# The three middle batches of a two-layer conditional kernel: one hardware loop, or the same code written out three times

## The chip, the cores and the metric

The kernel runs on one core of one Trainium2 chip. The metric is the device time of one execution in microseconds (us). A core has five instruction streams: PE (TensorE, matmuls), ACT (ScalarE), DVE (VectorE), POOL (GpSimd) and SP (SyncE, which here issues nearly all DMAs). Each stream runs in its own order and waits for the others by semaphores.

## What is computed

For each of 4 batches `x` is 1024 tokens x 512 features, float32. Cut to what matters:

```python
# layer 0: MLP whose last 128 output columns come from one of 16 experts, chosen per batch
h = gelu(x @ fc1_w.T + fc1_b)                    # 512 -> 2048
shared = h @ fc2_w.T + fc2_b                     # 2048 -> 384
expert = h @ experts_w[indices].T + experts_b[indices]   # 2048 -> 128
x = x + concat([shared, expert], -1)
# layer 1: attention pooling, mask chosen per batch by prompt type (prefix, postfix, all but self)
scores = tanh(x @ W1 + b1) @ v
p = softmax(where(mask, scores[:, None, :], NEG_INF), -1)
x = x + (p @ x) / count(mask)
```

## The kernel before, in words

Every float32 factor is split into a high part `hi` (ACT, a copy that rounds) and a remainder `lo` (DVE, a subtraction), and each product is three matmuls of 128x512 (`three`, L699 to L701). fc1 is computed in pairs of 128 hidden rows by a seven-product scheme. The seven products of a pair are P1, P5, P6, P3, P7, P2, P4; they are accumulated in two PSUM banks, `hA` and `hF`, which ACT copies out (`snap`), DVE adds to (`add`, L1278) and ACT puts through GELU (`gelu`, L926).

A batch has 8 pair steps (p = 0 to 7), in which PE does the fc1 products of pair p for the first token half and the second, and between them fc2 (`fc2`, bank `y`) for the hidden rows of the pair before, in eight groups of three matmuls; then 16 unit steps with fc2 alone for the second half. The attention of the batch before is spread over the pair steps as tasks. All four engines have a place for each task in tables written by hand (`POST_P`, `EX_P` and so on), and each engine's order is fixed by them.

The part that matters below is the expert weights. While batch b is computed, the expert matrix of batch b+1 is read in four quarters: SP issues the load into `exth` (`load_ex`, L398, 256 KB), ACT writes the high part to `Ph` (L872), DVE the low part to `Pl` (L1106), SP writes both to the DRAM buffer `exs` (`put_ex`, L406), and only then loads the next quarter. `EX_P` places the quarters in the loop at pair step 0, place 0; step 0, place 1; step 1, place 1; step 1, place 2. In each engine's order these tasks stand ahead of work of the pair itself: DVE's low part of quarter 0 ahead of the first `add` of step 0, ACT's high part of quarter 1 ahead of the third and fourth GELU of step 0, for which P1 of step 1 waits (`gelu_done`), and quarter 3 ahead of the copy of `hA` in step 2.

On SP these loads stand in one queue with the weight loads of the pairs (`load_w1`, L364) and of fc2 (`load_w2`, L368 and L369), and each of those waits until PE has finished with the buffer: before quarter 1 is put and the next loaded, SP waits in `gate` for the fourth fc2 group (group 3) of the pair step.

The program has three bodies: `first` (batch 0, with all weights split on the way), `loop` (batches 1 to 3) and `tail` (attention of the last batch). Before the change `loop` is one hardware loop whose counter `b` lies in a register of each engine: the value of nearly every wait in it, such as `b * 56 + 3`, is computed by register instructions, and so are the DRAM addresses with `b` in them.

Of the kernel before, what the change touches and what calls it, by code (L numbers as in the profile page):

```python
# [4 lines left out]
NB, SEQ, D = 4, 1024, 512  # L5
# [157 lines left out]
def build(nc, x, tok_e, tok_t, fc1_w, fc2_w, exp_w, exp_b, W1, biases, out):  # L163
# [7 lines left out]
    with ctx:  # L171
# [136 lines left out]
        def run(eng, part):  # L308

            part("first", 0)  # L310
            with eng.Fori(1, NB) as b:
                part("loop", b)
            part("tail", NB)

# [34 lines left out]
        def _(sp):  # L349
# [209 lines left out]
            for n in range(4):  # L559
                load_w2raw(n, e)  # L560
            run(sp, part)

            for i in range(OUTS):
# [11 lines left out]
        def _(pool):  # L575
# [75 lines left out]
            def part(kind, b):  # L651
# [31 lines left out]
                for p in range(PAIRS):  # L683
                    for k in range(3):
                        for task, pos in LOOP["p", p, k]:
                            if task[0] == "pool":
# [3 lines left out]
                                                        ALU.add).then_inc(row_sum, 1)  # L690

            run(pool, part)


        @block.tensor
        def _(pe):
# [153 lines left out]
            def part(kind, b):  # L850
# [9 lines left out]
                for u in range(HC):  # L860
                    for oc in range(OC):
                        fc2(kind, b, HC - 2 + u, oc)
                    for task, pos in BODIES[kind]["u", u, 0]:
                        job(kind, b, "u", task, pos)

            run(pe, part)


# [555 lines left out]
```

## Time and profile before

| | us |
|---|---|
| median of 3 runs | 875.6 |
| lowest, highest run | 871.32, 876.32 |
| time of the profiled execution | 868.85 |
| its span (first to last instruction) | 867.1 |
| PE busy in it | 799.7 (92%) |

The span of the profiled execution is the time from its first instruction to its last; 1.75 us of its time lie around it. The times of three executions differ by 0.6%, and the profiled one was below all of them. A busy PE is not a PE at its peak, since the ends of matmuls are modelled: in the stretches where nothing is waited for, a matmul of 512 columns follows the one before it every 0.227 us, though each is shown as 0.39 us long. In the trace batch 1 begins on PE at 185.0 us, batch 2 at 395.9, batch 3 at 607.05, and the last matmul of its fc2 is at 820.0.

### The profile page before, as it was taken

The page shows a single profiled execution, that of the slowest core. Times are in us where ns is not written, and L with a number is a line of the kernel's source. Part 1 is how long each engine was busy: PE and PEld are TensorE (multiplying, and loading weights), DVE is VectorE, ACT ScalarE, POOL GpSimd, SP SyncE. Part 2 cuts the span into 40 slices and gives each one's busy share as a digit, 9 for nine tenths or more (in the row PEclk, how much of TensorE's full clock was granted, in tenths as well). Part 3 has the DMA queues.
Part 4 walks back from the last instruction along what each step waited for, and adds up shares of the span by engine and source line. Part 5 has one row for each costly group of instructions (what it writes and reads, how often), then busy time and mean ns, then how long its engine had stood idle before and what let it go on. Part 6 is the DMA issues. An engine that isn't in the chain of part 4 may idle for free.

```text
span 867.1 us, 12247 instructions
## 1 busy us (share of the span) xinstructions
PE 799.7 (92%) x3550; PEld 648.0 (75%) x3550; DVE 399.1 (46%) x681; ACT 374.1 (43%) x621; POOL 104.9 (12%) x165
## 2 busy tenths in 40 slices
PE   6799999997799999997979999999797999999976
PEld 4677788875678888886758888887685888888755
DVE  6655558533343333761425333456143433275464
ACT  5755656423335434442435523443242553354222
POOL 3463110010000120002000021000200002100160
PEclk9999999998999999999989999999998999999968
DMA  8499988675544468866655447877564456786502
GB/s 265 149 358 356 290 292 276 211 216 185 180 148 135 158 206 282 269 185 214 184 142 169 150 159 235 290 214 219 184 196 145 134 168 209 228 270 210 179 0 98
DMA packets 130583, 176.80 MB, mean 204 GB/s; under 512 B 10048, under 2 KB 97616, under 8 KB 130512
## 3 DMA queue, kind: packets, MB, share of 16 engines
q1 hardware_dynamic: 130352, 175.94, 63.9%
q8 instruction: 33, 0.54, 0.3%
q14 instruction: 38, 0.31, 0.1%
q0 software_dynamic: 160, 0.01, 0.1%
HBM read 136.07 MB, written 39.85 MB: 203 GB/s over the span
## 4 chain that ended last, share of the span: by engine, by line
PE 79%; DMA 5%; DVE 4%; issue 4%; ACT 4%; SPq 3%; ACTq 0%; DVEq 0%
PE y L699 12%; PE y L701 12%; PE y L700 12%; PE hA L699 6%; PE hA L701 6%; PE hA L700 6%; PE hF L699 4%; PE hF L700 4%; PE hF L701 4%; DMA exth<-in_experts_w 4%; PE j L699 2%; PE j L700 2%; PE j L701 2%; PE j L769 1%; ACT gb L926 1%
## 5 line engine op out<-in xcount | busy, mean ns | idle before, releaser
L699 PE MATMUL y<-hs,w2c 128*128 128x512 f32 x512 | 202.7, 396 | 1.0 <-DVE w2c L1106 1.0
L701 PE MATMUL y<-hs,w2c 128*128 128x512 f32 x512 | 200.5, 392 | 0.0
L700 PE MATMUL y<-hs,w2c 128*128 128x512 f32 x512 | 200.5, 392 | 0.0
L699 PE MATMUL hA<-xch,w1c 128*128 128x512 f32 x252 | 103.1, 409 | 42.3 <-ACT gb L872 15.7
L699 PEld LDWEIGHTS y<-hs,w2c 128*128 128x128 f32 x512 | 97.0, 189 | 22.0 <-DVE hs L1106 1.4
L701 PEld LDWEIGHTS y<-hs,w2c 128*128 128x128 f32 x512 | 96.8, 189 | 20.7
L700 PEld LDWEIGHTS y<-hs,w2c 128*128 128x128 f32 x512 | 97.0, 189 | 19.7
L701 PE MATMUL hA<-xch,w1c 128*128 128x512 f32 x252 | 100.6, 399 | 0.0
L700 PE MATMUL hA<-xcl,w1c 128*128 128x512 f32 x252 | 100.6, 399 | 0.0
L699 PEld LDWEIGHTS hA<-xch,w1c 128*128 128x128 f32 x252 | 48.8, 194 | 58.1 <-issue 20.7
L699 PE MATMUL hF<-xch,w1c 128*128 128x512 f32 x190 | 77.4, 407 | 7.8 <-DVE hst L1278 7.8
L700 PE MATMUL hF<-xcl,w1c 128*128 128x512 f32 x190 | 76.0, 400 | 0.0
L701 PE MATMUL hF<-xch,w1c 128*128 128x512 f32 x190 | 76.0, 400 | 0.0
L1106 DVE TENSOR_TENSOR hs<-gb,hs 128x512 fp32r<-128x512 f32 x64 | 44.3, 693 | 67.4 <-ACT hs L872 67.4
L689 POOL TENSOR_TENSOR x1T<-x1T,xnl 128x512 f32<-128x512 f32 x24 | 30.8, 1286 | 355.0 <-DVE x1T L1224 355.0
L926 ACT ACTIVATE hst<-hst,bcol 128x512 f32<-128x512 f32 x62 | 43.3, 718 | 67.7 <-DVE hst L1278 67.7
L1106 DVE TENSOR_TENSOR hs<-hst,hs 128x512 fp32r<-128x512 f32 x64 | 44.1, 689 | 37.8 <-ACT hs L872 37.4
L872 ACT ACTIVATE hs<-hst 128x512 fp32r<-128x512 f32 x64 | 40.3, 629 | 48.1 <-PE y L701 48.1
L701 PEld LDWEIGHTS hA<-xch,w1c 128*128 128x128 f32 x252 | 48.7, 193 | 10.6
L700 PEld LDWEIGHTS hA<-xcl,w1c 128*128 128x128 f32 x252 | 48.9, 194 | 9.4
L1106 DVE TENSOR_TENSOR Pl<-exth,Ph 128x512 fp32r<-128x512 f32 x16 | 12.9, 806 | 83.5 <-ACT Ph L872 83.5
L926 ACT ACTIVATE gb<-gb,bcol 128x512 f32<-128x512 f32 x31 | 22.4, 724 | 66.0 <-DVE gb L1278 66.0
(232 smaller groups left out, 1104.8 us busy)
## 6 DMA issues: line engine op xcount, KB each, us to landing
w2c<-w2s SPq DMA_DIRECT2D x114, 384.0 KB, 3.4
w1c<-w1s SPq DMA_DIRECT2D x24, 768.0 KB, 4.3
w2c<-exs SPq DMA_DIRECT2D x114, 128.0 KB, 3.7
w1c<-w1s SPq DMA_DIRECT2D x48, 256.0 KB, 3.2
w1c<-w1s SPq DMA_DIRECT2D x24, 512.0 KB, 3.7
x1T<-in_x SPq DMA_DIRECT2D x32, 256.0 KB, 5.3
w1s<-w1c SPq DMA_DIRECT2D x8, 768.0 KB, 4.7
w2s<-w2c SPq DMA_DIRECT2D x16, 384.0 KB, 4.2
```

The lines of the kernel that those rows point to most:

```text
L689: nc.gpsimd.tensor_tensor(oo[:, c % OUTS, :], oo[:, c % OUTS, :], xnl[:, c, :].bitcast(f32), ALU.add).then_inc(row_sum, 1)
L699: nc.tensor.matmul(ps, ah, bh, start=first, stop=False, skip_group_check=onto)
L700: nc.tensor.matmul(ps, ah, bl, start=False, stop=False, skip_group_check=onto)
L701: return nc.tensor.matmul(ps, al, bh, start=False, stop=last, skip_group_check=onto)
L769: last = nc.tensor.transpose(bank[:, i * P:(i + 1) * P], x1T[:, i, c * P:(c + 1) * P], ident[:, :])
L872: return nc.scalar.activation(out_, in_, ACT.Copy)
L926: nc.scalar.activation(tile, hA[:, :] if order == 4 else tile, ACT.Gelu, bias=bcol[:, R_FC1 + m:R_FC1 + m + 1]).then_inc(gelu_done, 1)
L1106: return nc.vector.tensor_tensor(out_, in_, hi_.bitcast(f32), ALU.subtract)
```

## The change

The hardware loop over batches 1 to 3 is replaced by a Python loop. So `b` is a plain number while the program is built, the code of `loop` stands three times in each engine's stream, all its waits are for constants, and there is no jump from the end of a batch to the start of the next.

```diff
         def run(eng, part):
 
             part("first", 0)
-            with eng.Fori(1, NB) as b:
+            for b in range(1, NB):
                 part("loop", b)
             part("tail", NB)
```

Every engine calls `run` with its own `part`. What the diff doesn't tell is which instructions go. The names in the rows are the lines of the kernel; REGISTER_ALU and ISA are register and control instructions, and what stands in brackets is what the row waits for.

SP at the start of a loop pass: the last load of fc2 weights of the batch before, the type and expert number of the batch (L525, L423), and the load of quarter 0 of the expert (L398). Before:

```order
L369 DMA w2c<-exs 128x2x128
L311 UNCONDITIONAL_BRANCH
L311 ISA
L525 DMA ty<-in_itok_B_2 128x1
L423 TENSOR_LOAD in_itok_B_15_ptr
L423 ISA
L423 REGISTER_ALU
L423 TENSOR_LOAD in_itok_B_15
L423 ISA x2
L297 REGISTER_ALU
L398 ISA [waits exlo]
L398 DMA exth<-in_experts_w 128x512
```

After:

```order
L369 DMA w2c<-exs 128x2x128
L525 DMA ty<-in_itok_B_2 128x1
L423 TENSOR_LOAD in_itok_B_15_ptr
L423 REGISTER_ALU
L423 TENSOR_LOAD in_itok_B_15
L423 ISA x2
L398 ISA [waits exlo]
L398 DMA exth<-in_experts_w 128x512
```

No DMA has moved; the jump and the register work for the wait are gone, the two loads of the expert number from DRAM are still there.

SP in pair step 0, behind the fourth fc2 group (`fc2_done`): the fc2 weights, quarter 0 written out, quarter 1 loaded. Before:

```order
L368 DMA w2c<-w2s 128x2x384 [waits fc2_done]
L369 ISA
L369 DMA w2c<-exs 128x2x128
L297 REGISTER_ALU
L406 ISA [waits exlo]
L406 DMA exs<-Ph 128x4x128
L406 ISA
L406 DMA exs<-Pl 128x4x128
L398 ISA [waits exlo]
L398 DMA exth<-in_experts_w 128x512
```

After:

```order
L368 DMA w2c<-w2s 128x2x384 [waits fc2_done]
L369 DMA w2c<-exs 128x2x128
L406 DMA exs<-Ph 128x4x128 [waits exlo]
L406 DMA exs<-Pl 128x4x128
L398 ISA [waits exlo]
L398 DMA exth<-in_experts_w 128x512
```

The same five DMAs in the same order, with four register or control instructions fewer between them. The same piece stands in pair step 1 ahead of quarter 3.

ACT in pair step 0, from the second GELU on: quarter 1, third GELU, high part of the hidden rows, fourth GELU (for which PE waits), high part. Before:

```order
L926 ACTIVATE hst<-hst,bcol 128x512 [waits add_done]
L963 REGISTER_ALU
L872 ACTIVATE Ph<-exth 128x512 [waits ex_out1,ex_in]
L926 ACTIVATE gb<-gb,bcol 128x512 [waits add_done]
L940 REGISTER_ALU
L297 ISA [waits gelu_done]
L872 ACTIVATE hs<-gb 128x512 [waits fc2_done]
L924 REGISTER_ALU
L926 ACTIVATE gb<-hA,bcol 128x512 [waits hslo,fc1_done]
L940 REGISTER_ALU
L872 ACTIVATE hs<-gb 128x512 [waits fc2_done,gelu_done]
```

After:

```order
L926 ACTIVATE hst<-hst,bcol 128x512 [waits add_done] x2
L872 ACTIVATE Ph<-exth 128x512 [waits ex_out1,ex_in]
L926 ACTIVATE gb<-gb,bcol 128x512 [waits add_done]
L872 ACTIVATE hs<-gb 128x512 [waits fc2_done,gelu_done]
L926 ACTIVATE gb<-hA,bcol 128x512 [waits hslo,fc1_done]
L872 ACTIVATE hs<-gb 128x512 [waits fc2_done,gelu_done]
```

ACT does the same work in the same order; the register instructions between are gone.

## Rows read from the trace of the kernel before

**Rows 1.** Page, part 1 and part 3: engines' busy time; the two instruction queues.

```profile
PE 799.7 (92%) x3550; PEld 648.0 (75%) x3550; DVE 399.1 (46%) x681; ACT 374.1 (43%) x621; POOL 104.9 (12%) x165
...
q8 instruction: 33, 0.54, 0.3%
```

**Rows 2.** Timeline of PE: start, length, instruction, [idle before it, releaser].

```profile
195.35 0.49 PE L699 MATMUL hF<-xch,w1c 128*128 128x512 f32 x1 [0.66 <-DVE hst L1278]
...
207.32 0.80 PE L699 MATMUL hA<-xch,w1c 128*128 128x512 f32 x1 [6.24 <-ACT gb L926]
...
236.26 0.80 PE L699 MATMUL hA<-xch,w1c 128*128 128x512 f32 x1 [4.92 <-ACT gb L872]
...
395.88 0.49 PE L699 MATMUL hA<-xch,w1c 128*128 128x512 f32 x1 [1.08 <-issue]
...
409.56 0.79 PE L699 MATMUL hF<-xch,w1c 128*128 128x512 f32 x1 [3.89 <-DVE hst L1278]
...
418.33 0.50 PE L699 MATMUL hA<-xch,w1c 128*128 128x512 f32 x1 [1.70 <-ACT gb L926]
...
607.05 0.49 PE L699 MATMUL hA<-xch,w1c 128*128 128x512 f32 x1 [1.61 <-issue]
```

**Rows 3.** Chain of waits, at loop entries 2 and 3, and quarter 1's load.

```profile
197.75 5.17 DMA exth<-in_experts_w
...
396.36 3.16 issue
...
410.22 3.72 DMA exth<-in_experts_w
...
607.00 3.52 issue
```

**Rows 4.** Windows, steps 0-1, batches 1 to 3: length, busy; clock, DMA share, GB/s.

```profile
185.00:236.20 51.20, 39.44 (x168) 31.58 (x166) 15.09 (x24) 18.06 (x31) 5.13 (x11) 0.92 0.59 180
395.80:445.90 50.10, 39.16 (x167) 31.42 (x167) 15.33 (x24) 18.05 (x31) 4.81 (x11) 0.94 0.59 180
607.00:656.60 49.60, 39.45 (x167) 31.59 (x167) 15.14 (x24) 18.10 (x31) 5.08 (x11) 0.95 0.59 181
```

**Rows 5.** Timeline of SP, batch 0: constant addresses and waits.

```profile
59.19 0.74 SPq L380 DMA_DIRECT2D stageh<-in_experts_w  x1
60.05 0.40 SPq L406 DMA_DIRECT2D exs<-Ph  x1
60.50 0.50 SPq L406 DMA_DIRECT2D exs<-Pl  x1
61.25 0.37 SPq L398 DMA_DIRECT2D exth<-in_experts_w  x1
...
185.26 0.52 SPq L368 DMA_DIRECT2D w2c<-w2s  x1
185.83 0.61 SPq L369 DMA_DIRECT2D w2c<-exs  x1
```

**Rows 6.** Timeline of SP, batch 1: addresses and waits from registers.

```profile
194.79 0.56 SPq L368 DMA_DIRECT2D w2c<-w2s  x1
195.56 0.59 SPq L369 DMA_DIRECT2D w2c<-exs  x1
196.49 0.42 SPq L406 DMA_DIRECT2D exs<-Ph  x1
197.11 0.39 SPq L406 DMA_DIRECT2D exs<-Pl  x1
197.75 0.37 SPq L398 DMA_DIRECT2D exth<-in_experts_w  x1
```

**Rows 7.** Chain of waits, last `add` of a pair to P1: batch 0; then batch 2.

```profile
86.78 0.61 DVE gb L1278
...
89.53 0.47 PE hA L699
...
415.24 0.69 DVE gb L1278
```

## The prediction

> **What bounds the kernel now.** I read the page first: PE is busy for 92% of the span, no other engine for half of it [rows 1]. So a saving counts only where PE stands still, or where it lengthens or shortens something PE waits for. The next view is the timeline of PE with its idle times. In a whole pass of the loop (about 211 us) PE stands still for more than 0.6 us in few places only, and the reader is to see that all but the jump lie in pair steps 0 to 2 [rows 2]: in batch 1 0.66, 6.24 and 4.92 us; in batch 2 1.08 at the loop's start with no releaser ("issue": the jump), then 3.89 and 1.70; batch 3 begins with 1.61 of the same kind. Outside these places the matmuls follow each other every 0.227 us, in the loop with its register instructions as in batch 0 without. So PE's own register instructions cost nothing there: its queue hides them, and I count 0 for them.
>
> What PE waits for in steps 0 to 2 the chain of waits tells: a quarter of the next expert's weights, queued by SP behind fc2 weights, ahead of GELU and copies on ACT. Batch 1 is the piece to study, because it is entered from the straight code of batch 0: it has no jump on any engine, and so shows what batches 2 and 3 will be like.
>
> **The jump on PE.** It costs 1.08 + 1.61 = 2.7 us of idle [rows 2] and goes for certain. Whatever matmul is next is ready: its operands have been there since the batch before. Term: **-2.7 us**.
>
> **The jump on SP.** In the chain of waits SP loses 3.16 and 3.52 us at its two jumps [rows 3], between the last fc2 load and the load of quarter 0. This is the larger number, and the first thing to settle is whether it is paid. Before, quarter 0 lands late, DVE's low part holds up the `add`, and PE waits 3.89 us for it in batch 2; quarter 1 follows when that is through, with a second wait of 1.70. Without the jump, as batch 1 shows, the first wait is 0.66, but the second is 6.24 [rows 2]. The sum of the two is no smaller. The reason is SP's order: quarter 1 may be loaded only after the gate on the fourth fc2 group, on PE's own progress, and then come two fc2 loads and two writes of quarter 0 [rows 6]. Quarter 0 early doesn't bring quarter 1 forward by more than a little, and the transfer itself took 5.17 us in batch 1 against 3.72 in batch 2 [rows 3], because in batch 2 the weight loads of this stretch had drained while SP waited. So SP's 6.7 us are nearly all cover, behind which the next wait stands. To put a number on it I compare the lengths of steps 0 and 1 together, jumps left out: 51.2 us in batch 1, 50.1 and 49.6 in batches 2 and 3 [rows 4]. They include the half-speed matmuls that follow a wait: the granted clock, at 0.92, is lowest in batch 1. If batches 2 and 3 become like batch 1, they get longer by 1.1 and 1.6. Term: **+2.7 us**.
>
> The price of a jump on this chip is then what the rows show, 1.1 to 3.5 us. The Trainium skill has two rules that would make it different things. "Advanced Engine Details and Errata", Control Flow Timing, gives a branch about 51 ns; "Runtime: NRT & Kernel Launch", Instruction fetch mechanics, says that a taken branch out of the prefetched pages waits for a DMA fetch of its target. By the first the jump terms would be 0.1 us in all instead of 2.7, and the idle on PE would still be there afterwards. The trace's idle times agree with the second.
>
> **Register work on SP between the fourth fc2 group and quarter 1.** It is serial on the queue that sets the wait, so it counts. Constant against register, starts of DMA issues: L368 to L369 0.57 against 0.77; idle from the DMA ahead of `put_ex` to its first issue 0.12 (59.93 to 60.05) against 0.34 (196.15 to 196.49); L406 to L406 0.45 against 0.62; L406 to L398 0.75 against 0.64, here the register form is the faster [rows 5, 6]. Sum: 0.20 + 0.22 + 0.17 - 0.11 = 0.48 us. The same piece stands ahead of quarter 3 in step 1, whose wait is the 4.92 us in batch 1. Two per batch, three batches: 6 x 0.48 = 2.9. Term: **-2.9 us**. Bounds: 0, if the DMAs drain no sooner because the queues are full, and 6 x 0.8 if each gap falls to the smallest that the constant rows show (0.05).
>
> **Register work on ACT and DVE in that chain.** From the start of the last `add` to the start of P1: 86.78 to 89.53 = 2.75 us in batch 0, whose waits are constants, and 415.24 to 418.33 = 3.09 in batch 2 [rows 2, 7]. The same operations, so 0.34 us is register work, once per batch: **-1.0 us**. Behind quarter 3 ACT goes through several register instructions too, but the engine is then at its own pace, with one copy after the other, and I count 0. Bounds for the whole of ACT and DVE: 0 to 2.2 us, the latter with 0.34 at the second wait and the same again over the task work.
>
> **No cost that I can find** in the rest: no DMA is moved or added, the two loads of the expert number from DRAM stay, POOL and DVE stand still around their jumps anyway, and waits that now sit on the instruction were there before as separate ones. Code bytes: the instruction queue of 16 KB pages took 33 packets in the whole span [rows 1], loop passes are fetched again now, so the written-out code fetches about the same bytes, and in one line.
>
> **The sum.** -2.7 + 2.7 - 2.9 - 1.0 = -3.9 us: 868.85 to 864.95 for the profiled execution. The median of the runs shown, 875.6, is 6.75 above that execution; the change takes the same from both, so I predict **871.7 us**. The runs differ by 5 us and about 1% is what a measurement of this kernel can tell from no change, so I expect it to be called the same. With the terms at their bounds (register work 0 to 7.0 us, quarter 1's transfer landing from 5.17 as in batch 1 to 3.72 as in batch 2, twice, which is another -2.9) the result is between 875.6 and 865.7.
>
> **Rivals.**
>
> *SP's jump is paid in full.* If quarter 0's arrival is what the end hangs on, each batch saves what SP saves: -(3.16 + 3.52) - 3.9 = -10.6 us, 865.0, faster by 1.2%. For it: PE's 3.89 us name exactly this chain. Against it: batch 1, where the first wait is gone and the second has grown. It needs quarter 1 to land early too and the half-speed stretch behind the wait to vanish. 0.13.
>
> *Nothing but an exchange.* The register work is hidden, by DMA queues that are busy for 59% of these steps [rows 4] and by engines that work off their queues; then jump and longer steps cancel and the time is 875.6. For it: the exchange is seen in the rows, while the register terms are compared between different places of the program, one of which came out the other way round. 0.16.
>
> *Instruction fetch of the straight code, the slow side.* The place is PE's stream. The loop's pages now come for the second and third pass at other moments and other addresses, 33 pages of 16 KB over the span, so some 8 per batch, 16 in the two batches written out. If a page comes late, PE stalls for about what the jump costs, (1.08 + 1.61) / 2 = 1.35 us. All of them late: 16 x 1.35 = 21.6 us, less 3.9: 893.3, slower by 2%. It decides from three late pages on (4.0 us), where the gain is used up. Against it: batch 0 and the first pass are straight code with the same pages, and PE has no idle time without a releaser in them after the first 26 us. 0.05.
>
> *Quarter 1 lands later than in batch 1.* With SP faster by 0.48 us it goes out sooner behind the same weight loads; if what SP gains is lost in the transfer, half the register term goes (+1.5 us): inside the forecast.
>
> **How the numbers follow.** The forecast, a gain of 1 to 8 us, gets 0.63; nothing 0.16; SP's jump in full 0.13; late pages 0.05; the rest, 0.03, is for a day on which both kernels run elsewhere. The range for 8 in 10 goes from the full jump to just above the exchange, with the scatter of the medians (0.3% or so) on the upper side: 864.5 to 877. More than 1% faster means below 866.8: the rival at 865.0 and the lowest edge of the forecast, 0.16. More than 1% slower, above 884.4, takes ten or more late pages: 0.04 with the unexplained rest. The same: 0.80.
>
> **What the profile after should show.** No PE idle by "issue" at the starts of batches 2 and 3, and batch length equal in all three. In steps 0 and 1 of batches 2 and 3 the first wait at 0.7 to 1.8 us and the second at about 5.4 (6.24 less 0.8), so that these steps look like batch 1; the third at about 4.4. From the fourth fc2 group to the issue of quarter 1 2.5 us on SP instead of 3.0. From the last `add` to P1 2.75 instead of 3.09. If the second wait stays at 1.7 with the first near zero, the first rival is right; if it is still 6.2 with SP's issues closer together, the second; idle by "issue" in the middle of a batch would be the third. The prediction is wrong if the transfer of quarter 1 doesn't behave as in batch 1, or if the wait depends on something that this trace hides behind the jump.

## The result, and the profile after

The written-out kernel takes 876.68 us (median of 17 runs, 873.64 to 881.4), the kernel before in runs beside them 873.38 us (17 runs, 870.67 to 879.09). The ratio is 1.0037 with a 95% interval of 1.0019 to 1.0055: slower by 0.4%, less than 1% but clear of no change. I had forecast a gain of 3.9 us; the loss is 3.3 us. The time lies at the upper end of the range that I gave, the sign is wrong. That it lies in the range at all is luck: I started from 875.6 us, the median of three runs, and the kernel before came out 2.2 us lower in 17. From 873.38 us the same reasoning gives 869.5 us and a range of 862.3 to 874.8, and the measured time lies above that.

The profiled execution took 878.05 us, with a span of 876.4. It says first that the program did become shorter and PE's work did not: 10690 instructions instead of 12247, the same 3550 matmuls, busy 809.5 us instead of the 799.7 of [rows 1] because more of them ran at the lower clock. From the page, engines and the instruction queue:

```profile
span 876.4 us, 10690 instructions
...
PE 809.5 (92%) x3550; PEld 657.1 (75%) x3550; DVE 398.2 (45%) x681; ACT 373.9 (43%) x621; POOL 104.5 (12%) x165
...
q8 instruction: 29, 0.48, 0.2%
```

The 16 KB instruction pages went down from 33 to 29: no more fetching than before.

The timeline of PE, at the places of [rows 2] (start, length, instruction, idle before it and releaser), batches 1, 2 and 3:

```profile
208.45 0.77 PE L699 MATMUL hA<-xch,w1c 128*128 128x512 f32 x1 [6.96 <-ACT gb L926]
...
238.29 0.77 PE L699 MATMUL hA<-xch,w1c 128*128 128x512 f32 x1 [5.17 <-ACT gb L872]
...
410.08 0.47 PE L699 MATMUL hF<-xch,w1c 128*128 128x512 f32 x1 [0.20 <-issue]
...
421.96 0.77 PE L699 MATMUL hA<-xch,w1c 128*128 128x512 f32 x1 [6.16 <-ACT gb L926]
...
451.01 0.76 PE L699 MATMUL hA<-xch,w1c 128*128 128x512 f32 x1 [5.20 <-ACT gb L872]
...
631.51 0.76 PE L699 MATMUL hA<-xch,w1c 128*128 128x512 f32 x1 [6.91 <-ACT gb L926]
```

There is no idle at the starts of batches 2 and 3 any more. In batch 2 the waits of 3.89 and 1.70 us have become 0.20 and 6.16: batches 2 and 3 look like batch 1, as forecast. But the waits themselves are longer than I wrote down: the second 6.16 us in batch 2 instead of about 5.4, the third 5.17 and 5.20 instead of about 4.4. And batch 1 itself, which had no jump before and has only lost its register work, waits 6.96 instead of 6.24 us.

The windows of [rows 4] (length; busy time of PE, PEld, DVE, ACT, POOL; granted clock, DMA share, GB/s). They reach from P1 of step 0 to the end of the third wait, which lies inside step 2, a little further than I said there:

```profile
185.70:238.30 52.60, 40.05 (x169) 32.12 (x167) 15.46 (x24) 18.22 (x31) 4.86 (x11) 0.90 0.60 176
400.20:451.00 50.80, 39.24 (x168) 31.52 (x167) 15.24 (x24) 18.20 (x31) 4.75 (x11) 0.92 0.61 181
609.20:661.70 52.50, 40.15 (x168) 32.20 (x167) 15.23 (x24) 18.20 (x31) 4.97 (x11) 0.89 0.59 174
```

They are longer than before in all three batches, by 1.4, 0.7 and 2.9 us, at a lower granted clock (0.90, 0.92, 0.89 against 0.92, 0.94, 0.95). Now the timeline of SP in batch 1, for [rows 6], and behind it from the chain of waits the two transfers of quarter 1 that answer to [rows 3]:

```profile
195.46 0.55 SPq L368 DMA_DIRECT2D w2c<-w2s  x1
196.06 0.60 SPq L369 DMA_DIRECT2D w2c<-exs  x1
196.76 0.54 SPq L406 DMA_DIRECT2D exs<-Ph  x1
197.35 0.50 SPq L406 DMA_DIRECT2D exs<-Pl  x1
198.10 0.38 SPq L398 DMA_DIRECT2D exth<-in_experts_w  x1
```

```profile
198.10 6.23 DMA exth<-in_experts_w
...
412.61 5.24 DMA exth<-in_experts_w
```

From the first issue behind the gate to quarter 1's issue it is 2.64 us where it was 2.96; I had forecast 2.5. But the transfer takes 6.23 us where it took 5.17, so the quarter is there 8.9 us after the gate instead of 8.1. The saving on the queue is real, and in this profile it is worth nothing.

One profile of each kernel can mislead here, as the next section shows: the profiled execution before, 868.85 us, was faster than any of the runs of that kernel above.

### The profile page after: what moved, and what is told of

Its sections match the earlier page's. It is cut to its first block, busy times and chain, and to the rows that moved or that the text cites. A ratio compares the mean times of both kernels' runs of the same rounds, so it can differ in the third digit from the quotient of the medians.

```text
span 876.4 us, 10690 instructions
## 1 busy us (share of the span) xinstructions
PE 809.5 (92%) x3550; PEld 657.1 (75%) x3550; DVE 398.2 (45%) x681; ACT 373.9 (43%) x621; POOL 104.5 (12%) x165
## 4 chain that ended last, share of the span: by engine, by line
PE 82%; DMA 5%; DVE 4%; ACT 4%; issue 3%; SPq 2%; ACTq 0%; DVEq 0%
PE y L699 12%; PE y L701 12%; PE y L700 12%; PE hA L699 7%; PE hA L701 6%; PE hA L700 6%; PE hF L699 5%; PE hF L700 4%; PE hF L701 4%; DMA exth<-in_experts_w 4%; PE j L699 2%; PE j L700 2%; PE j L701 2%; PE j L769 1%; ACT gb L926 1%
## 5 line engine op out<-in xcount | busy, mean ns | idle before, releaser
L699 PE MATMUL hA<-xch,w1c 128*128 128x512 f32 x252 | 104.2, 413 | 48.8 <-ACT gb L926 22.8
L699 PEld LDWEIGHTS y<-hs,w2c 128*128 128x128 f32 x512 | 97.2, 190 | 21.7 <-issue 1.1
L701 PE MATMUL hA<-xch,w1c 128*128 128x512 f32 x252 | 102.0, 405 | 0.0
L699 PE MATMUL hF<-xch,w1c 128*128 128x512 f32 x190 | 78.5, 413 | 0.7 <-issue 0.6
L701 PE MATMUL hF<-xch,w1c 128*128 128x512 f32 x190 | 76.7, 404 | 0.0
L926 ACT ACTIVATE gb<-gb,bcol 128x512 f32<-128x512 f32 x31 | 22.4, 724 | 70.6 <-DVE gb L1278 70.6
```

The costliest lines, as they stand in the source:

```text
L699: nc.tensor.matmul(ps, ah, bh, start=first, stop=False, skip_group_check=onto)
L701: return nc.tensor.matmul(ps, al, bh, start=False, stop=last, skip_group_check=onto)
L926: nc.scalar.activation(tile, hA[:, :] if order == 4 else tile, ACT.Gelu, bias=bcol[:, R_FC1 + m:R_FC1 + m + 1]).then_inc(gelu_done, 1)
```

## The experiments

Two theories stood at the start. **A**: the loss comes from SP. Without its jump quarter 0 goes out early, quarter 1 goes into a queue full of weights, and one long wait takes the place of two short ones. **B**: the loss comes from PE's written-out code. In the profile after, pair step 4 took 23.6 us in batches 1 and 3 instead of 20.3, its matmuls 0.43 us apart instead of 0.227, after a wait of 0.62 us at the denominator (L812).

### 1 and 2: one engine with the loop, the others without

```diff
-        def run(eng, part):
+        def run(eng, part, written_out=False):
             part("first", 0)
-            with eng.Fori(1, NB) as b:
-                part("loop", b)
+            if written_out:
+                for b in range(1, NB):
+                    part("loop", b)
+            else:
+                with eng.Fori(1, NB) as b:
+                    part("loop", b)
             part("tail", NB)
...
-            run(sp, part)
+            run(sp, part, True)      # run 1; run 2: True for pool, pe, act, dve instead
```

> Only SP's loop is written out, PE, ACT, DVE and POOL keep the hardware loop with its jumps and register waits. Theory A (the loss comes from SP: quarter 0 goes out early, quarter 1 is queued behind the weight loads still in flight, and one long wait of 6 to 7 us with a longer half-speed stretch takes the place of two short ones): slower than before by 0.3 to 0.7%, with the long second wait in batches 2 and 3 and the idle at PE's jumps still there. Theory B (the loss comes from PE's side: more half-speed stretches after the short wait at the denominator in pair step 4, whatever SP does): within 0.2% of before.

> PE, ACT, DVE and POOL written out, SP keeps its loop and jumps. Theory A: quarter 0 stays late in batches 2 and 3 (waits near 3.9 and 1.7 us as before), the idle of 1.1 and 1.6 us at PE's jumps is gone, though part of it may come back in the first wait: faster than before by 0.2 to 0.5%. Theory B: slower than before by 0.4%, like the kernel with everything written out, with low-clock stretches at pair step 4 in most batches.

Run 1 measured 1.0013 (0.9989 to 1.0038), run 2 1.0002 (0.9975 to 1.0030). As totals both are inconclusive. A missed both ranges (0.3 to 0.7% slower, 0.2 to 0.5% faster); B's "within 0.2%" holds for run 1 and its "0.4% slower" does not for run 2. The timelines are clearer. PE in run 1, where only SP is written out, batches 2 and 3:

```profile
397.49 0.49 PE L703 MATMUL hA<-xch,w1c 128*128 128x512 f32 x1 [1.05 <-issue]
...
420.61 0.80 PE L703 MATMUL hA<-xch,w1c 128*128 128x512 f32 x1 [7.87 <-ACT gb L930]
...
610.44 0.49 PE L703 MATMUL hA<-xch,w1c 128*128 128x512 f32 x1 [2.14 <-issue]
...
635.10 0.80 PE L703 MATMUL hA<-xch,w1c 128*128 128x512 f32 x1 [7.81 <-ACT gb L930]
```

SP alone makes the long wait, 7.87 and 7.81 us, behind PE's jumps of 1.05 and 2.14 us. PE in run 2, where SP keeps its jump, batch 2:

```profile
409.60 0.76 PE L703 MATMUL hF<-xch,w1c 128*128 128x512 f32 x1 [4.56 <-issue]
...
418.76 0.47 PE L703 MATMUL hA<-xch,w1c 128*128 128x512 f32 x1 [1.87 <-ACT gb L930]
```

Here are the two short waits of before again, at the same two matmuls. The first is longer because PE no longer jumps and is there earlier. The profile names no releaser for it ("issue"), in run 2 and in run 3 below, but it is not a jump: it stands at the first matmul into `hF` of step 0, where the first profile names DVE's `add`. The shape of the waits is SP's doing; the price of the shape was not settled by these two.

### 3: SP held back as by the jump

```diff
                 if p == 0:
+                    if b > 1:
+                        sp.wait_ge(fc1_done, products(b, 0, P3))
                     load_ex(b, 0, e1)
```

> Everything written out; in batches 2 and 3 SP holds the load of quarter 0 until PE has done product P3 of pair step 0, which is about when it went out after the jump. Theory A: waits of about 4 and 1.7 us in those batches as before, transfer of quarter 1 back to about 4 us, faster than the written-out kernel by 3 us or more and than before by 0.1 to 0.5%. Theory B: as slow as the written-out kernel, 0.4% above before.

Measured 0.9958 (0.9935 to 0.9980) of the kernel before: faster than it, and the interval lies clear below that of the written-out kernel. It differs from the latter by one wait on SP in two batches. PE, and the transfers from the chain of waits, batch 2:

```profile
410.13 0.65 PE L701 MATMUL hF<-xch,w1c 128*128 128x512 f32 x1 [4.23 <-issue]
...
419.22 0.47 PE L701 MATMUL hA<-xch,w1c 128*128 128x512 f32 x1 [1.77 <-ACT gb L928]
```

```profile
403.43 4.62 DMA exth<-in_experts_w
410.70 4.40 DMA exth<-in_experts_w
```

The waits are 4.23 and 1.77, the transfer of quarter 1 is back at 4.4 us. The windows from P1 to the end of the third wait are 51.2 and 51.0 us in batches 2 and 3. So a load that is issued about 3 us later makes the kernel faster, which speaks for A and rules out that SP's jump is paid in full. The 3.7 us by which the median ratio lies under 1 is near what PE's jumps cost. This run is also the best total test of my register terms: with the waits of batches 2 and 3 left in their old shape I should have had -2.7 - 2.9 - 1.0 = -6.6 us, and the interval reaches from -1.7 to -5.7 us.

### 4: the denominator one place later

```diff
-... (4, 0): [("expPW", 1)], (4, 1): [("den", 0, CH), ("pool", 0)], (4, 2): [("pool", 1)],
+... (4, 0): [("expPW", 1)], (4, 2): [("den", 0, CH), ("pool", 0), ("pool", 1)],
```

> Everything written out; the denominator and the first pooling product of pair step 4 moved one place later (place 2 instead of 1) on all engines, so that PE does not wait 0.6 us for the exponentials there. Theory A: the long waits in pair step 0 stay, at most 1 us is gained by the wait itself, 0.2 to 0.4% above before. Theory B: the half-speed stretches in pair step 4 (3.3 us each in batches 1 and 3 of the written-out kernel) are gone, 3 to 7 us faster than the written-out kernel, so 0.1 to 0.4% below before.

Measured 1.0008 (0.9978 to 1.0038). Step 4 took 21.0 us in all three batches, with no stretch at half speed, but a wait of 1.23 us in each. The interval overlaps with that of the written-out kernel and with 1: inconclusive, and taken up again in run 11.

### 5 and 6: the quarters at other places of the loop

```diff
-EX_P = [(0, 0), (0, 1), (1, 1), (1, 2)]
+EX_P = [(0, 1), (1, 0), (1, 2), (2, 1)]
```

> The hardware loop as before; the four quarters of the next expert are taken at other places of the loop: pair step 0 place 1, step 1 place 0, step 1 place 2, step 2 place 1, so that each has a good half of a pair step more to land. Theory A (PE waits for transfers of quarters, and these waits decide what the jump is worth): the waits of 4 to 7 us in step 0 and of 5 us in step 2 shrink to under 2 us, and with them the half-speed stretches: faster than before by 3 to 5% (25 to 40 us). Theory B (the quarters only happen to stand last, and the waits move to the next thing in the queue): within 1% of before.

> The same places for the quarters, with everything written out. Theory A: SP's jump no longer matters since nothing waits for quarter 0, so what is left of the change is the idle at PE's two jumps: 2.5 to 4 us below the same kernel with the loop (0.3 to 0.45%). Theory B (written-out code on PE has a cost of its own, half-speed stretches in pair step 4): not faster than the same kernel with the loop.

With the loop: 829.05 us (827.56 to 830.93), ratio 0.9453 (0.9422 to 0.9485). Written out: 826.47 us (825.2 to 827.4), ratio 0.9423 (0.9393 to 0.9453). The waits of PE from the start of batch 1 to the end of batch 3 (engine, line, releaser: us in total, times, longest). Before:

```profile
PE hA L699 <- ACT gb L872: 15.7, 3, 5.4
PE hA L699 <- ACT gb L926: 9.4, 3, 6.2
PE hF L699 <- DVE hst L1278: 7.8, 3, 3.9
PE hA L699 <- issue: 2.7, 2, 1.6
```

The written-out kernel:

```profile
PE hA L699 <- ACT gb L926: 20.0, 3, 7.0
PE hA L699 <- ACT gb L872: 15.8, 3, 5.4
```

Moved quarters with the loop:

```profile
PE hA L699 <- issue: 2.9, 2, 1.5
PE j L699 <- DVE xnl L1106: 1.7, 2, 1.0
PE j L812 <- DVE Ws L1106: 1.6, 3, 0.5
```

Moved quarters, written out:

```profile
PE j L812 <- DVE Ws L1106: 1.9, 3, 0.6
PE j L699 <- DVE xnl L1106: 1.6, 3, 0.9
```

Nearly 33 us of waits, and the half-speed matmuls behind them, were the price of where the quarters stood; A's range was 3 to 5%, and it is 5.5%, so A undershot. With them gone, the change of this study is worth what it removes from PE: the line "issue" 2.9 us goes, and the medians differ by 2.6 us. This is also the version that beats both kernels. The Trainium skill, "Runtime: NRT & Kernel Launch", Instruction fetch mechanics, has a taken branch wait for its target page; these two runs agree that PE stands still at each of its two jumps, for about 1.5 us; that it is a page it waits for, no run here shows.

### 7, 8 and 12 to 15: the two kernels again

> The kernel before once more, for a second profile: shows which of the half-speed stretches of the first profile come back. Theory A: pair steps 0 and 1 of batches 2 and 3 within 1 us of the first profile. Theory B: pair step 4 at 20.2 us in at least two batches of three.

> The written-out kernel once more, for a second profile. Theory A: one long wait in pair step 0 of all three batches, steps 0 and 1 together 42 to 44 us. Theory B: pair step 4 at 23.6 us in two batches of three again.

> A third profile of the kernel before. If the half-speed stretches in pair step 4 are chance, about one batch in two to three has one in either kernel; if written-out code sets them off, none or one here and two or three in the written-out kernel. From the fourth fc2 group's gate to quarter 1 in SBUF about 8.6 us in batch 1, as in the written-out kernel, if the transfer takes back what the issue gains.

> A third profile of the written-out kernel: pair step 4 as in the run before this one if chance, two or three stretches if the code sets them off; gate to quarter 1 in SBUF 8.5 to 8.9 us in all batches.

> A fourth profile of the kernel before, with the same expectations as the third.

> A fourth profile of the written-out kernel, with the same expectations as the third.

With the first profiles that makes four of each kernel. From the starts of matmuls in their timelines, means of four, in us:

| stretch | before | written out | difference | forecast |
|---|---|---|---|---|
| batch 0, to the start of batch 1 | 185.17 | 185.46 | +0.3 | 0 |
| steps 0 and 1, batch 1 | 43.44 | 43.36 | -0.1 | -0.8 |
| steps 0 and 1, batches 2 and 3 | 42.45, 41.70 | 43.50, 43.76 | +3.1 | +1.1 |
| step 2, three batches | 26.88, 26.76, 27.12 | 26.85, 27.38, 27.57 | +1.0 | -1.4 |
| step 4, three batches | 21.51, 21.10, 20.71 | 22.36, 21.15, 21.15 | +1.3 | 0 |
| step 7 and second half with the jump, batches 1 and 2 | 65.82, 65.74 | 64.32, 64.33 | -2.9 | -2.7 |
| last fc2 to the last matmul | 43.99 | 44.86 | +0.9 | 0 |
| sum | | | +3.6 | -3.9 |

The forecast for steps 0 to 2 is the +2.7, -2.9 and -1.0 of the prediction, laid out over the rows; rounding hides 0.1. Measured in 17 runs each: +3.3.

Of what I had expected of the second profiles, A's "within 1 us" failed: steps 0 and 1 of batches 2 and 3 took 42.8 us each before, not 41.1 and 40.5. B's step 4 held for the kernel before (20.3 us in all three batches) and failed for the written-out one (22.0, 20.4 and 20.3 instead of 23.6 twice). Of the third and fourth, the way from the gate to quarter 1 in SBUF was 8.0 and 8.3 us in batch 1 before, not about 8.6, and 7.8 to 9.1 us over all batches after, not 8.5 to 8.9.

For quarter 1 in batch 1, where the two kernels differ by register work alone: from the first issue behind the gate to its own issue 2.96 to 2.97 us before and 2.64 to 2.65 after; from the issue to the start of ACT's copy of it 5.19, 6.11, 5.02, 5.34 before and 6.26, 5.86, 5.19, 6.45 after; together 8.4 on average before and 8.6 after. The single values lie within 0.8 us of these means, so four against four don't settle it, but runs 1 to 4 have the same piece: 9.2, 9.4 and 8.7 us where SP is written out (runs 1, 3 and 4), 8.4 where it isn't (run 2). None of this looks like a gain of 0.3. For quarter 3 in step 1, the other half of the term, the same way takes 7.40 us before and 7.34 after (means of 12 batches each), and the third wait is 5.34 and 5.37 us.

What the transfer of quarter 1 meets can be read from windows laid over it alone, batch 1 of the first profiles, before and after (the last three numbers are granted clock, DMA share and GB/s):

```profile
197.75:202.95 5.20, 3.33 (x15) 2.44 (x13) 0.00 (x0) 0.01 (x1) 0.00 (x0) 1.00 0.85 241
198.10:204.30 6.20, 3.39 (x15) 2.46 (x14) 0.00 (x0) 0.00 (x0) 0.00 (x0) 0.93 0.99 269
```

In the four profiles of each kernel the 16 DMA engines were busy during this transfer for a share of 0.84 to 0.91 before and 0.96 to 1.00 after in batch 1, and for 0.79 to 0.90 (3.7 to 5.1 us) against 0.90 to 1.01 (5.2 to 6.5 us) in batches 2 and 3. So in the written-out kernel quarter 1 is loaded by DMA engines that are busy nearly all the time.

Step 4 ran partly at half speed in 5 of 12 batches before and in 5 of 12 after, for longer after (23.6 us against 21.9, mostly). The spread is 1.1 and 1.6 us per batch, so the sum over three batches is known to about 1.7 us (estimate from that spread), and +1.3 is no difference that these profiles show. B's forecast, none or one against two or three in a profile, isn't borne out.

### 9: quarter 1 ahead of the fc2 weights

```diff
                     if k == 0:
                         load_w1(b, p, 1)
+                        if p == 0:
+                            put_ex(b, 0)
+                            load_ex(b, 1, e1)
 
                         gate(sp, fc2_done, units(b, 2 * p - 2, OC, OC))
...
-                    if (p, k) in EX_P:
+                    if (p, k) in EX_P[1:]:
```

> Everything written out, places of the quarters as in the first two kernels; in pair step 0 SP writes out quarter 0 and loads quarter 1 ahead of the fc2 weights instead of behind them. Theory A (quarter 1 lands late because it stands behind 512 KB of weights and 512 KB written out, so what the constant addresses save at the issue is lost in the transfer): issue about 1.5 us sooner, transfer 4 to 5 us instead of 5.3 to 6.3, second wait 3 to 5 us instead of 6 to 7.5, so 5 to 12 us faster than the written-out kernel (0.4 to 1.0% below before). Theory B (a transfer from the experts' array takes 6 us at this place whatever is ahead of it): only the issue counts, 1.5 us per batch, 3 to 5 us faster than the written-out kernel.

Measured 0.9917 (0.9879 to 0.9954), 7.3 us below the kernel before and 10.5 below the written-out one by the ratios. SP in batch 1, and the transfer from the chain of waits:

```profile
193.51 0.37 SPq L406 DMA_DIRECT2D exs<-Ph  x1
193.93 0.50 SPq L406 DMA_DIRECT2D exs<-Pl  x1
194.68 0.40 SPq L398 DMA_DIRECT2D exth<-in_experts_w  x1
195.19 1.05 SPq L368 DMA_DIRECT2D w2c<-w2s  x1
```

```profile
194.68 5.43 DMA exth<-in_experts_w
...
405.61 5.79 DMA exth<-in_experts_w
```

The issue is 2.0 us sooner after P1 than in the written-out kernel (10.4 us against 12.4), the second wait 4.38, 4.75 and 5.01 us instead of 6.96, 6.16 and 6.91. The transfer is 5.4 to 6.1 us, not the 4 to 5 that A gave: it no longer stands behind the fc2 weights but with them beside it, and gets no shorter by that. So what is ahead of it isn't the whole story, and A is right on the place and on the total, and too simple on the mechanism; B had the transfer right (about 6 us) and the total wrong. The DMA engines were busy for 0.91 to 0.94 during these three transfers, which points to everything in flight in those microseconds and not to what is ahead in the queue alone; no run here varies that by itself.

### 10 and 11: does PE's written-out code have a price of its own?

```diff
+            run(eng, part, True)      # run 10: sp, pool, act and dve, not pe; quarters as in run 5
...
+... (4, 2): [("den", 0, CH), ("pool", 0), ("pool", 1)],      # run 11: as run 4, quarters as in run 6
```

> Quarters at the new places; SP, ACT, DVE and POOL written out, PE keeps its loop and its jumps. Theory A (with the quarters out of the way only PE's jumps are left of the change): the same time as the moved quarters with the whole loop, 2 to 3 us above the written-out one. Theory B (PE's constant waits cost half-speed stretches in pair step 4): jumps cost 2.9 us, stretches give back 1 to 3 us, within 1 us of the written-out one.

> Quarters at the new places, everything written out, and the denominator one place later as in the fourth run. If the half-speed stretches of pair step 4 are set off by the short wait there: step 4 at 21.0 us in all three batches instead of 22.0, 23.6 and 21.9, so 0.5 to 4 us faster than the written-out kernel with moved quarters. If they come by chance of the clock: a stretch falls elsewhere, and the fixed 0.8 us per batch makes it 1 to 2.5 us slower.

Run 10: 831.92 us (829.26 to 833.07), ratio 0.9484 (0.9447 to 0.9520): 5.4 us above the kernel with everything written out. B wanted it within 1 us; step 4 took 23.6, 20.4 and 22.0 us although PE runs the loop. B falls. It is also 2.9 us above run 5, though, where A wanted the same; one batch waits 2.0 us in step 1 for the input of the attention product (`xnl`), and the intervals overlap. In the two profiles 2.2 of the 2.4 us between them lie in batch 0, which neither change touches (batch 1 begins at 186.7 us against 184.5). The rest stays open.

Run 11: 826.55 us, ratio 0.9424 (0.9384 to 0.9465), the same as run 6 to 0.1 us. Step 4 took 21.7, 22.4 and 21.0 us, so the half-speed stretches fall a little later instead of going away. The wait at the denominator isn't their one trigger.

## Why the prediction was wrong, point by point

**What bounds the kernel**: right. All of PE's waits that matter were those of [rows 2], and moving what they hang on gave 5.5%.

**The jump on PE, -2.7 us**: right: -2.9 in the mean of four profiles, -2.6 between runs 5 and 6.

**The jump on SP, worth nothing and exchanged for +2.7 us**: right in kind and nearly in size. Batches 2 and 3 came to look like batch 1: steps 0 and 1 take 43.5 and 43.8 us where batch 1 of the kernel before takes 43.4. They grew by 3.1 us in all. In batch 2 of the first profile before the two fc2 loads went out from 4.5 us ahead of quarter 1, in batch 1 from 3.0 us, which fits my reason for the shorter transfer, that their data had drained. Run 1 gives the long wait with SP alone written out, run 3 takes it away by holding SP alone. The rival that counted 6.7 us for SP's jump is refuted by run 3: holding back the load is a gain.

**The register work on SP, -2.9 us**: this is the step that failed. I summed 6 x 0.48 us as "serial on the queue that sets the wait, so it counts". The issue did come 0.32 us sooner per place (less than 0.48 mainly because the issue of the first write of quarter 0 lasts 0.54 us here and 0.40 in batch 0). But what PE waits for is the arrival, and 0.3 us on the issue are given back by the transfer: 8.4 us from gate to arrival before, 8.6 after, in batch 1, where no jump differs, and 7.40 against 7.34 for quarter 3. So the term measures about nothing instead of -2.9, which run 3 bears out in the total. I had named this as a bound ("0, if the DMAs drain no sooner because the queues are full") and as a case inside the forecast, and took the other end without a row for it. The DMA share of 0.59 in [rows 4] could not tell, being a mean over 50 us; over the transfer alone it was 0.85 before, and is 0.99 after. Why quarter 3 gains nothing either, with the engines busy for only 0.71 to 0.85 during its transfer, is not settled.

**The register work on ACT and DVE, -1.0 us**: the handoff from the last `add` to P1 went from 3.11 to 2.82 us in batch 1 (205.63 to 208.45 in the profile after), and from 3.09 to 3.11 down to 2.82 in all twelve batches of each kernel, so 0.3 per batch as forecast, and this is about the -0.1 that batch 1 gained in the end, with the 0.2 that the arrival lost.

**What I left at 0**: step 2, the tail and batch 0 came out 1.0, 0.9 and 0.3 us longer. Step 2 grew in batches 2 and 3 alone, and not by its wait, which is 5.43 us on average in these batches before and 5.48 after: the rest of the step went from 21.5 to 22.0 us, matmuls that ran at the lower clock behind the wait. For the reason I have no run. The others, like step 4, show no more than the scatter of half-speed stretches.

**The rival "nothing but an exchange"**, 875.6 us at 0.16, was nearest, though its reason, that the jump terms cancel and the register work is hidden, is only most of the story: by the table the places of the two jumps give +0.2, batch 1 another -0.1, and the interval of the measured ratio excludes 0. I gave it the small chance because two terms with rows looked firmer than one bound without. The fetch of straight code cost nothing that the trace shows: no idle by "issue" over 0.5 us in the loop, 29 pages.

What remains between this 0 and the measured +3.3 (interval +1.7 to +4.8) is made of step 2, step 4, the tail and batch 0. The last three lie within their scatter; step 2 of batch 3 hardly does (26.9 to 27.5 us before, 27.4 to 27.7 after). So it is shown that the change gives back nearly all that it takes from PE's jumps, and that my register term on SP is worth nothing; why the kernel comes out slower, and not equal, is not settled.

## What to carry to other kernels

Time removed from a queue ahead of a transfer counts only if the transfer arrives sooner; read the arrival, not the issue, and look at what is in flight beside it. A stall on a queue can be doing the work of a schedule: when it goes, the loads behind it meet traffic that had drained while it lasted, so find out first what it kept apart. And the wait that a change only reshapes is worth more than the change: here four places in a table gave 48 us, the loop 2.6.

## What the runs showed of the hardware

At the end of nearly all waits of 2.6 to 7.9 us in these profiles the granted clock is at its lower level, with matmuls 0.43 us apart instead of 0.227. It falls also in the middle of step 4 behind an idle of 0.5 to 0.6 us, in some executions and not in others of the same kernel; the runs go with it: of the 17 of the written-out kernel the five at a granted clock of 0.957 took 873.6 to 875.7 us, the one at 0.945 881.4.

The back edge of the loop cost 0.8 to 2.1 us of idle on PE over all profiles with PE in the loop, and 3.2 and 3.5 us on SP in the first one, at the same two places of the program. Between SP's last fc2 load and its next DMA the written-out kernel stands still for 0.05 us there (first profile, end of batch 1).

A 256 KB load from the same array took from 3.3 to 6.7 us from issue to arrival. In run 9 quarter 0 took 3.4 to 3.5 us with the DMA engines busy for 0.45 to 0.48 of that time; quarter 1, six microseconds later, 5.4 to 6.1 at 0.91 to 0.94.
